# A GRU scan on one core: the n gate in three bf16 parts, r, z and n apart by halves

## The reference, cut to what matters

```python
def cell(h, x):                    # h (4, 512), one of 512 time steps
    gi = x @ W_ih + b_ih           # known for all steps ahead of time
    gh = h @ W_hh + b_hh           # 512 x 1536, needs the last step's h
    i_r, i_z, i_n = split(gi, 3); h_r, h_z, h_n = split(gh, 3)
    r = sigmoid(i_r + h_r)
    z = sigmoid(i_z + h_z)
    n = tanh(i_n + r * h_n)
    return (1.0 - z) * n + z * h   # the new h
```

## Time and profile before

| | |
|---|---|
| median of 3 runs | 2115.24 us (2114.27 to 2116.45) |
| profiled execution, from its first to its last instruction | 2113.7 us |
| PE, PEld, DVE, ACT, POOL busy | 98%, 75%, 64%, 59%, 30% |
| TensorE's granted clock | 0.997 |
| the 512 steps | from 572.4 to 2105.5 us |

### The profile page before, as it was taken

The page is one execution under the profiler, slowest core; times in us unless marked ns, Lnnn a source line. Parts: engine busy times, 40 slices in busy tenths (PEclk is TensorE's granted clock), DMA queues, the critical chain, the costliest instruction groups (busy, mean ns, idle before and its releaser), DMA issues.

```text
span 2113.7 us, 181503 instructions
## 1 busy us (share of the span) xinstructions
PE 2071.9 (98%) x77848; PEld 1578.9 (75%) x77848; DVE 1354.9 (64%) x6162; ACT 1239.1 (59%) x5995; POOL 638.0 (30%) x1015
## 2 busy tenths in 40 slices
PE   8999999999999999999999999999999999999998
PEld 2222222222499999999999999999999999998887
DVE  4344445444367777777777777777777777776676
ACT  3445544443266666666666666666666666666665
POOL 0355547444112222222222222222222222222222
PEclk9999999999999999999999999999999999999999
DMA  6000000011222222221222222222121212210001
GB/s 259 1 1 1 1 1 1 1 60 31 49 54 53 52 55 52 52 55 49 69 59 55 52 53 53 56 58 66 50 58 50 58 48 60 67 30 11 5 8 20
DMA packets 218082, 96.04 MB, mean 45 GB/s; under 512 B 170216, under 2 KB 213480, under 8 KB 217320
## 3 DMA queue, kind: packets, MB, share of 16 engines
q1 hardware_dynamic: 217032, 92.00, 16.8%
q10 hardware_dynamic: 928, 2.65, 0.3%
HBM read 26.30 MB, written 12.58 MB: 18 GB/s over the span
## 4 chain that ended last, share of the span: by engine, by line
PE 70%; DVE 2%; issue 0%; DMA 0%; ACT 0%; SPq 0%; DVEq 0%
PE ps L1241 64%; PE ps L1274 4%; PE ps L1282 2%; DVE arena L1069 1%; DVE arena L1087 0%; DMA arena<-arena 0%; DVE arena L965 0%; DVE arena L1075 0%; DVE arena L1082 0%; DVE arena L968 0%; ACT arena L1210 0%; SPq L994 0%; DVE arena L1158 0%; DVE seq L1163 0%; DVE seq L1100 0%
## 5 line engine op out<-in xcount | busy, mean ns | idle before, releaser
L1241 PE MATMUL ps<-whh,arena 128*4 128x128 f32 (+1 forms) x65568 | 1451.4, 246 | 13.8 <-issue 1.6
L1241 PEld LDWEIGHTS ps<-whh,arena 128*4 128x4 f32 x65568 | 1293.6, 87 | 112.2 <-DVE arena L1087 25.8
L1069 DVE STREAM_TRANSPOSE arena<-ps 128x64 f32<-128x64 f32 x2048 | 446.4, 284 | 256.1 <-PE ps L1241 237.0
L1199 ACT ACTIVATE arena<-arena 128x8 f32<-128x8 f32 x1024 | 216.1, 211 | 543.4 <-DVE arena L1069 480.1
L455 DVE TENSOR_REDUCE top<-ps 128x2 f32<-128x1024 f32 x128 | 150.8, 1220 | 244.0 <-PE ps L722 244.0
L1174 ACT ACTIVATE ps<-arena 128x128 f32<-128x128 f32 x1026 | 288.9, 282 | 0.5 <-PEq L212 0.4
L1087 DVE TENSOR_TENSOR_SCAN arena<-arena 128x24 f32<-128x24 f32 x1024 | 192.1, 188 | 145.1 <-ACT arena L1210 145.1
L1075 DVE STREAM_TRANSPOSE arena<-ps 128x64 f32<-128x64 f32 x1024 | 257.5, 251 | 9.0 <-PE ps L1241 3.3
L361 ACT ACTIVATE arena<-ps 128x1024 f32<-128x1024 f32 x128 | 124.1, 1021 | 212.7 <-PE ps L798 212.6
L610 PE MATMUL ps<-arena 128*32 128x512 f32 x2048 | 242.7, 595 | 2.7 <-ACT arena L383 2.7
L965 POOL TENSOR_TENSOR arena<-tap,arena 128x128 f32<-128x128 f32 x252 | 102.0, 415 | 430.0 <-DVE seq L1100 430.0
(11 more groups left out here) (99 smaller groups left out, 1268.0 us busy)
## 6 DMA issues: line engine op xcount, KB each, us to landing
arena<-arena SPq DMA_DIRECT2D x216, 114.0 KB, 2.2
arena<-arena SPq DMA_DIRECT2D x112, 128.0 KB
arena<-seq SPq DMA_DIRECT2D x224, 55.0 KB
arena<-gi_d SPq DMA_DIRECT2D x248, 32.0 KB
gi_d<-arena SPq DMA_DIRECT2D x96, 57.0 KB
out<-seq SPq DMA_DIRECT2D x14, 256.0 KB
seq<-in_x SPq DMA_DIRECT2D x3, 1024.0 KB, 15.6
whh<-in_w_hh SPq DMA_DIRECT2D x1, 3072.0 KB, 21.1
```

The costliest lines, as they stand in the source:

```text
L1069: e.transpose(trn[:, h, q].rearrange("p (i c s) -> p c i s", c=2, s=2)[:, :, :, 0], bank[RN[h]][:, 64 * q:64 * q + 64].rearrange("p (c i) ...
L1199: e.activation(r_d0[:, h].rearrange("p (i s) -> p i s", s=2)[:, :, 1], trn[:, h, 0, 0:2 * NH].rearrange("p (i s) -> p i s", s=2)[:, :, 0], ...
L1241: last = e.matmul(bank[dst[h]][32 * G:32 * G + B, 0:n], hv, wv[:, k, gates, G, 64 * h:64 * h + 64], start=False, stop=k2 == 1 and k == C - ...
```

## The change

Four things change together.

First, r and z stay f32 but are made apart, 64 columns each; n is made from bf16. The n columns of `W_hh` are split on GpSimd, during attention, into three bf16 parts whose sum is the f32 value. The new state is split each step on VectorE: a state value is read as bf16 by its upper 16 bits, `rest` subtracts that from the value, and so twice more or less (`second`, `third`); the three parts lie 3 floats apart. `products_n` loads 16 columns (4 batches by 3 parts and a column of zeros) as weights and streams 64 columns for each of the three parts of the matrix. The partial sums by part of the state come out in separate rows; `scan_n` adds them up, so that it runs over 40 elements.

Second, TensorE's order: `begin` makes r of both output halves, z of half 0 and n of half 0, all from state half 0. `end` makes r, z and n of half 0 from state half 1, then n of output half 1 whole, then its r, then its z.

Third, VectorE gets four small subtractions a step, and `gate_op` (the fetches for `part`) moves from behind the step to a place between `second(0)` and `third(0)`.

Fourth, the input products come in narrower and more frequent pieces: 57 columns (`AW`), bodies of two steps (224 of them), with one chunk of `W_in` for n at a time.

```diff
+PARTS = 3
-        whh = sb("whh", [P, C, 3 * D])
+        whh = sb("whh", [P, C, 2 * D])
+        whn = sb("whn", [P, D])
+        wn3 = sb("wn3", [P, C, PARTS, D], BF16)
+        bhn = sb("bhn", [P, P])
...
+        HS, HW = 3 * NH, PARTS + 1
+        NS5 = PARTS + 2
...
+        def rest(e, u, h, part):
+
+            return e.tensor_tensor(h_of(u, h, part + 1), h_of(u, h, part), top_of(u, h, part), ALU.subtract)
...
+        SPLITS, SPLIT_OPS = (2, 3, 6, 7), 2 * PARTS - 1
...
+                for k in range(C):
+                    if k:
+                        e.wait_ge(g_whn, SPLIT_OPS * k)
+                    e.dma_start(whn[:], w_hn[:, D * k:D * k + D]).then_inc(s_whn, 16)
...
+                        e.dma_start(bhn[32 * g + HW * b:32 * g + HW * b + 1, :], v.rearrange("(a n) -> a n", a=1)).then_inc(s_bhn, 16)
...
+                def split_weights(k):
+
+                    wait(s_whn, 16 * k + 16)
+                    for i in range(PARTS):
+                        if i:
+                            wait(g_whn, SPLIT_OPS * k + 2 * i - 1)
+                            e.tensor_tensor(whn[:], whn[:], wn3[:, k, i - 1], ALU.subtract).then_inc(g_whn, 1)
+                            wait(g_whn, SPLIT_OPS * k + 2 * i)
+                        e.tensor_copy(wn3[:, k, i], whn[:]).then_inc(g_whn, 1)
...
+                    if n in SPLITS:
+                        split_weights(SPLITS.index(n))
...
-        AW, NW = 114, 55
+        AW, NW = 57, 55
-        BODIES = 2 * len(N_BLOCKS)
+        BODIES = C * len(N_BLOCKS)
...
-                    turn_rn(0)
+                    def second(h):
+                        e.wait_ge(st["s_h"], h_half[h])
+                        rest(e, 1 - u, h, 0).then_inc(st["s_top"], 1)
+
+                    def third(h):
+                        e.wait_ge(st["s_top"], half[h])
+                        rest(e, 1 - u, h, 1).then_inc(st["s_p"], 1)
+
+                    turn_r(0)
                     turn_z(0)
+                    turn_n(0)
                     scan_n(0)
-                    turn_rn(1)
+                    turn_r(1)
+                    turn_n(1)
                     scan_h(0)
                     turn_z(1)
                     scan_n(1)
+                    second(0)
+                    gate_op()
+                    third(0)
                     scan_h(1)
+                    second(1)
+                    third(1)
...
+                def gate_ops(t):
+
+                    q, v = divmod(t, 2)
+                    if v == 1 and q < BODIES:
+                        take_rz(q)
+                    if v == 0 and q % C == 0 and 0 < q <= BODIES:
+                        take_n(q // C - 1)
+                        if q < BODIES:
+                            seed_n(q // C)
...
                         reset(0)
-                        seed_rn(0, s)
+                        seed_r(0, s)
+                        e.wait_ge(st["s_tz"], half[0])
+                        seed_z(0, s)
                         update(0)
                         new(0)
+                        e.wait_ge(st["s_tn"], half[0])
+                        seed_n(0)
                         reset(1)
-                        seed_rn(1, s)
+                        seed_r(1, s)
                         update(1)
                         new(1)
+                        e.wait_ge(st["s_tn"], half[1])
+                        seed_n(1)
+                        bring(following)
+                        e.wait_ge(st["s_tz"], half[1])
                         seed_z(1, s)
...
+                def products_n(u, h, k2, stop):
+
+                    for k in (2 * k2, 2 * k2 + 1):
+                        hv = parts_of(u, k)
+                        for s in range(PARTS):
+                            for G in range(NG):
+                                last = e.matmul(bank[N[h]][32 * G:32 * G + HW * B, 0:64], hv, wp[:, k, s, G, 64 * h:64 * h + 64],
+                                                start=False, stop=stop and k % 2 == 1 and s == PARTS - 1, skip_group_check=True)
...
                     e.wait_ge(st["s_h"], half[0])
-                    e.wait_ge(st["s_seed_rn"], half[0])
-                    products(u, RN, rn, 0, 0)
-                    e.wait_ge(st["s_seed_rn"], half[1])
-                    products(u, RN, rn, 1, 0)
+                    e.wait_ge(st["s_seed_r"], half[0])
+                    products(u, R, 0, 0, 0)
+                    e.wait_ge(st["s_seed_r"], half[1])
+                    products(u, R, 0, 1, 0)
+                    e.wait_ge(st["s_seed_z"], half[0])
+                    products(u, Z, 1, 0, 0)
+                    e.wait_ge(st["s_p"], half[0])
+                    e.wait_ge(st["s_seed_n"], half[0])
+                    products_n(u, 0, 0, False)
...
                     e.wait_ge(st["s_h"], half[1])
-                    products(u, RN, rn, 0, 1).then_inc(st["s_rn"], 1)
-                    e.wait_ge(st["s_seed_z"], half[0])
-                    products(u, RZ, z, 0, 0)
-                    products(u, RZ, z, 0, 1).then_inc(st["s_z"], 1)
-                    products(u, RN, rn, 1, 1).then_inc(st["s_rn"], 1)
+                    products(u, R, 0, 0, 1).then_inc(st["s_r"], 1)
+                    products(u, Z, 1, 0, 1).then_inc(st["s_z"], 1)
+                    e.wait_ge(st["s_p"], half[1])
+                    products_n(u, 0, 1, True).then_inc(st["s_n"], 1)
+                    e.wait_ge(st["s_seed_n"], half[1])
+                    products_n(u, 1, 0, False)
+                    products_n(u, 1, 1, True).then_inc(st["s_n"], 1)
+                    products(u, R, 0, 1, 1).then_inc(st["s_r"], 1)
                     e.wait_ge(st["s_seed_z"], half[1])
-                    products(u, RZ, z, 1, 0)
-                    products(u, RZ, z, 1, 1).then_inc(st["s_z"], 1)
+                    products(u, Z, 1, 1, 0)
+                    products(u, Z, 1, 1, 1).then_inc(st["s_z"], 1)
```

More of the change, by code:

```diff
@@ L1056, in _, with step @@
             def _(e):
[L1057 removed]
+                def step(t, u, gate_op):
                     def count(v):
@@ L1183, in _ @@
                 for h in range(2):
-                    seed_rn(h, 0)
-                for h in range(2):
+                    seed_r(h, 0)
+                    seed_n(h)
                     seed_z(h, 0)
@@ L1309, in _ @@
                 with e.Fori(0, BODIES) as it:
[L1310 to L1311 removed]
+                    for v in range(2):
+                        end(it * 2 + v, v)
                         part(v, it)
[L1313 to L1314 removed]
+                        begin(it * 2 + v + 1, 1 - v)
+                with e.Fori(BODIES, T // 2) as it:
                     for v in range(2):
```

230 lines of the change are left out of this document (112 added, 118 removed).

## The result

The changed kernel takes 2289.84 us (median of 4 runs, 2285.46 to 2291.06) against 2115.47 for the kernel before: ratio 1.0819, 95% interval 1.0806 to 1.0832. It is slower by 174 us where 14 less were forecast. The profiled execution has a span of 2287.1 us.

A forecast was written before the change was run, and what follows sets the result against it. The prediction took a loop through TensorE and `scan_h(0)`, not TensorE's busy time alone, as the bound. Step -42, `gate_op` +5 and +21, first bodies +2 sum to -14: 2115.2 becomes 2101 us, range 2068 to 2230.

The forecast's parts named there:

- the issue order costs nothing: TensorE's matmul groups: issue order was taken as free, and so was changing between f32 and bf16.
- a bf16 group of 64 columns at 0.029: n on TensorE: four one-pass matmuls take 0.029 us with weight loads hidden; 24 groups make 0.70 us a step.
- Rival (b): n's bf16 groups take 0.056, bound by issue or weight loads: about 3.45 us a step, some 2390; chance 0.12.
- The slack of the working: New schedule, TensorE: z half 1 ends 1.42, slice about 1.72, `begin` starts 1.75, after `scan_h(0)` ends at 1.70.
- Good step 2.89: The new step: 2.88 us plus 0.01 lost at `third(1)`, 0.08 less per step, times 512: -42 us.
- rival (a): VectorE's state split sets the pace: subtractions at 0.27 instead of 0.19 start n 0.16 later, 2183; chance 0.19.
- `take_rz`, `take_n`, `seed_n` at 26: `gate_op` between `second(0)` and `third(0)`: `take_rz` +5 us over 216 times, `take_n` and `seed_n` +21 over 56.
- Rival (c): `gate_op` on VectorE costs nothing because VectorE's waits are longer than reckoned: 2075; chance 0.10.
- 40-element scans at 0.24: `scan_n` on VectorE: 40 elements instead of 16, at 2 ns per element, takes 0.24 us.
- The slices "in an idle stretch": Slices of input products cost nothing, lying in TensorE's idle 0.33 us per step that waits for `scan_h(0)`.
- Loads by SP hidden: SP's loads land 2 us later, needed 3 us later: hidden; without that cover up to 2 us a body.
- Rival (d): Small waits in VectorE's fixed order bring the step back to 2.94, so no shortening: 2115 to 2125; chance 0.16.

The follow-up runs named there:

- experiment 5: Changed kernel with TensorE's loop beginning with `begin` and closing behind the slice, bf16 matmuls cut from 64 to 32 columns, half of n left out: 2256.44 us.
- experiment 9: Changed kernel, loop closing behind the slice, with two or one of the matrix's three bf16 parts, rest of n left out: 2115.11 and 2038.74 us.
- turning: Changed kernel with TensorE's loop body beginning with `begin` and closing behind the slice, nothing else changed: 2260.13 us, ratio 1.0679 to the kernel before.
- experiment 3: Changed kernel, loop closing behind the slice, with `gate_op`'s fetches moved behind the whole step: 2250.13 us, ratio 1.0632 to the kernel before.
- experiment 4: Changed kernel, loop closing behind the slice, GpSimd's convolution instructions cut from 128 columns to one: 2255.58 us, ratio 1.0664 to the kernel before.
- experiment 7: The kernel before with only the changed kernel's slices (57 columns, two-step bodies throughout): 2128.28 us, ratio 1.0057 to the kernel before.

## Why the prediction was wrong

**The step that failed is the price of TensorE's issue**: "the issue order costs nothing", a bf16 group of 64 columns at 0.029, with its weight loads taken as hidden, and no term at all for TensorE's sequencer, though the change doubles the closings of its loop. In the runs:

- A group takes 0.036 on average, from 0.65 us for 72, with 64 columns or with 32 (experiment 5), or about 8.9 ns a pair. The 0.029 holds only as long as pairs lie ready: for the 24 of `begin`, and for about the first six groups of the 72. The two n stretches take 0.65 + 0.19 where 0.70 stood: 0.14 a step, 72 us over 512. The formula "columns at 2.4 GHz plus 0.0025" was read from 128-column rows at 14 ns a pair, where the array is slower than the issue, and so could not show it. Rival (b) had the place and the kind right and its size too large (0.056); its own chance was 0.12.
- The loop's end is exposed: 0.40 us a body, 102 us over 256, from the timeline after. In the kernel before it lay under f32 matmuls of 128 columns, and half as often.

The two come to 174 us, against a miss of 2290 - 2101 = 189. They are readings of the trace, and experiments bear each of them out. The pairs: the third part costs its whole 8.8 ns for each of 32 pairs (145 us, experiment 9). The loop's end: turning takes the step without slices from 3.20 to 3.02. That turning gave back only 30 of the 102 is because, with slices, `begin` then starts 0.27 late behind each loop's end, 61 us in all. The common cause is that at 96 pairs a step TensorE's sequencer is hardly ahead of the matmuls, so that what it has to do besides shows: at 32 pairs the same loop's end, the same slices and the same VectorE work fit into 2.73 to 2.83 us a step. The slack of the working, on the other hand, held as long as nothing else stood in it: z half 1 ending at 1.42 and the slice at 1.72 for a `begin` at 1.75 are 0.03 us to spare, and in the changed kernel `begin` does start 0.055 behind `scan_h(0)` in both kinds of steps (median). It had no room for a loop's end, in whose place the working had nothing.

The Trainium skill ("TensorE: Matmul & The Clock Gate", section "Back-to-back issue gap") had said that the load counts too in such a stream. The 32-column run agrees that more than the columns counts. But the first groups of a stretch are 0.029 apart with their loads beside them, so it is not the load by itself. Its 81 ns per matmul at 128 columns is not what four column groups show here: 0.056 for four.

**Point by point.**
- f32 groups of 64 columns at 0.056: right (0.67 for 48 records).
- Good step 2.89: measured 2.96 at best, 3.01 on average without slices. With 0.14 more for n it should be 3.03; that subtractions of 0.167 instead of 0.19 pay a part back is likely and not shown.
- Subtractions as the pace, rival (a): wrong; 7.8 us of matmuls' waits for them in all.
- `take_rz`, `take_n`, `seed_n` at 26: moving them gave 10 (experiment 3). Rival (c), that they are free, was wrong as well.
- 40-element scans at 0.24: right on average; that some are held by GpSimd was not in the working. Taking GpSimd's work away gave 4.5 us in the turned kernel, which is not clear of the noise (experiment 4).
- The slices "in an idle stretch": they cost the kernel before 12.5 us in their new form (experiment 7).
- Loads by SP hidden: no wait for a DMA is among TensorE's rows of waits in the loop.
- Rival (d), that the shortening doesn't come: it went past that.
- The range's upper end, 2230, came from leaving out the full rival (b), the one with the right mechanism; half of it belonged inside.
- Two sums of the working are slightly off: 8 x 2 x 0.109 and 16 x 0.056 are 2.64, not 2.62, and rival (d)'s 2.94 with 28 gives 2128. The failure doesn't come from them.

**What stays open.** In half of the steps with slices an n stretch of 72 bf16 records lasts about 0.15 longer, within itself, with nothing that the profile names as releaser. Timeline of the turned kernel, such a stretch (0.80 from start to start) and the one of the next step (0.65):

```profile
1501.00 0.99 PE L1322 MATMUL ps<-wn,arena 128*16 128x64 bf16 x71
1501.80 0.88 PE L1312 MATMUL ps<-whh,arena 128*4 128x64 f32 x48
...
1504.48 0.84 PE L1322 MATMUL ps<-wn,arena 128*16 128x64 bf16 x72
1505.13 0.87 PE L1312 MATMUL ps<-whh,arena 128*4 128x64 f32 x48
```

I have not found why. Nor was it measured how the 0.27 by which `begin` is late in the turned kernel divides between the loop's end and the register waits of the slices. A version with the reference's precision that beats the kernel before was not found: the best with all of n is 2220 us; two parts of the matrix tie with it, one part is 3.7% faster, and both leave out part of the matrix.

## What to carry to other kernels

Before splitting an f32 matmul into bf16 parts, count instructions as well as columns: in a stretch of 72, a pair of load and matmul cost 8.9 ns whether it was 64 or 32 columns wide, and twelve pairs in place of four two-pass matmuls bought nothing. Then add up what an engine has to take in per step, its loop's end and its waits on registers included, and see what slack is left: work that "lies in the idle stretch" costs its price once the stretch is full. The quickest test of such a bound is to take away a third of the instructions and see whether the time falls by exactly their price.

## What the runs showed of the hardware

- Pairs of weight load (16 columns) and bf16 matmul of 64 columns over four column groups start 7.1 to 7.4 ns apart, 0.029 us for four, when they are few or at the head of a stretch. Over a stretch of 72 they average 8.9 ns, and the same with 32 columns (0.65 and 0.64 us).
- The end of TensorE's loop exposes 0.40 us when 24 bf16 pairs stand before it and 0.28 when 8 do; under f32 matmuls of 128 columns it does not show. The compare-and-branch in it lasts 0.207 us.
- A loop body of 1792 records of matmuls and loads (without slices) is fetched anew in each pass and more than doubles the time (5001.74 us, 21.30 MB on the instruction queue); the bodies of 1024 of the kernel before are not (47 packets).
- A scan with two inputs in SBUF that starts while a GpSimd instruction has some time left lasts until about 0.1 us after that one ends (0.52 us where the mean is 0.249). The Trainium skill ("SBUF — State Buffer", section "🔬 SBUF: two separate sides") has this as a port pair that the two engines share and lock for a whole instruction; the trace agrees, and with GpSimd's instructions cut to one column no scan lasts over 0.3 us.
